# Reordering the tail of a two-block pair kernel: where the last triangle, the output gates and the scaled projection stand

## The reference, cut to what matters

```python
zn = _sparse_norm(z, alpha_in, beta_in)
a = sigmoid(_lin(zn, W_ga, b_ga)) * _lin(zn, W_la, b_la)
b = sigmoid(_lin(zn, W_gb, b_gb)) * _lin(zn, W_lb, b_lb)
k = jnp.einsum('bitc,bjtc->bijc', a, b)
kn = _sparse_norm(k, alpha_o, beta_o)      # one mean, one variance over all of k
return sigmoid(_lin(zn, W_go, b_go)) * _lin(kn, W_lo, b_lo)
...
x = x + _L1_conv_ref(_gn(x), ...)
```

## Time and profile before

| what | value |
|---|---|
| median of three runs | 309.21 us (308.65 to 311.91) |
| time of the profiled execution | 310.55 us |
| its span in the profile | 308.5 us |
| PE / DVE / ACT / POOL busy, share of the span | 80% / 77% / 69% / 64% |
| matmuls and other instructions in all | 8141 |

### The profile page before, as it was taken

The page is one execution under the profiler, slowest core; times in us unless marked ns, Lnnn a source line. Parts: engine busy times, 40 slices in busy tenths (PEclk is TensorE's granted clock), DMA queues, the critical chain, the costliest instruction groups (busy, mean ns, idle before and its releaser), DMA issues.

```text
span 308.5 us, 8141 instructions
## 1 busy us (share of the span) xinstructions
PE 246.4 (80%) x3337; PEld 145.8 (47%) x3342; DVE 237.5 (77%) x444; ACT 214.3 (69%) x393; POOL 196.4 (64%) x174
## 2 busy tenths in 40 slices
PE   3965774889799799799799799795972698979983
PEld 1442251464465455455455554563611245555662
DVE  3997979688998998998996896895867574422784
ACT  4766785699699689689688788593723366755390
POOL 8907888889989889889849727329085862000053
PEclk9995899899999999999999999998996599999999
DMA  7201022023031031031041033100000026455016
GB/s 245 67 0 55 16 78 62 0 62 78 2 102 36 2 97 45 3 102 36 2 104 36 0 100 83 29 2 3 0 2 0 1 50 149 128 140 146 12 50 222
DMA packets 32576, 18.14 MB, mean 59 GB/s; under 512 B 21084, under 2 KB 29596, under 8 KB 32540
## 3 DMA queue, kind: packets, MB, share of 16 engines
q1 hardware_dynamic: 32540, 17.63, 21.1%
HBM read 8.18 MB, written 5.77 MB: 45 GB/s over the span
## 4 chain that ended last, share of the span: by engine, by line
DVE 41%; PE 32%; ACT 11%; issue 6%; DMA 4%; POOL 3%; SPq 1%; DVEq 0%; ACTq 0%
PE PS L1181 29%; DVE t_sb L934 5%; DVE nmax L949 5%; DVE og L909 5%; DVE S_sb L953 4%; ACT u_sb L619 3%; DVE sums L870 3%; DVE gn_part L1018 2%; DVE Z L1171 2%; DVE PP L914 2%; ACT t_sb L633 2%; DMA k_dram<-og 2%; DMA x_tok<-in_x 1%; DVE xT L899 1%; DMA PP<-u_sb 1%
## 5 line engine op out<-in xcount | busy, mean ns | idle before, releaser
L1181 PE MATMUL PS<-znT,A_bd 128*128 128x512 f16 x192 | 49.1, 402 | 14.2 <-DVE t_sb L934 12.2
L440 POOL TENSOR_TENSOR S_sb<-S_sb,rden 128x512 f32<-128x512 f32 x32 | 35.5, 1132 | 24.3 <-DVE rden L889 24.3
L934 DVE TENSOR_TENSOR t_sb<-PS,t_sb 128x512 f16<-128x512 f32 x64 | 41.0, 685 | 10.7 <-ACT t_sb L633 10.7
L633 ACT CAST t_sb<-PS 128x512 f16<-128x512 f32 x64 | 36.3, 611 | 16.0 <-PE PS L1181 14.9
L446 POOL TENSOR_TENSOR PP<-S_sb,PP 128x512 f16<-128x512 f32 x32 | 36.5, 1159 | 6.5 <-ACT PP L627 6.5
L1181 PEld LDWEIGHTS PS<-znT,A_bd 128*128 128x128 f16 x192 | 17.6, 102 | 44.6 <-DVE t_sb L934 25.0
L1181 PEld LDWEIGHTS PS<-PP,Z 128*128 128x128 f16 x512 | 29.3, 114 | 12.9 <-issue 12.0
L619 ACT COPY u_sb<-PS 128x512 f32<-128x512 f32 x64 | 32.7, 613 | 1.7 <-PE PS L1181 1.7
L1181 PE MATMUL PS<-zbd,t_sb 128*128 128x64 f16 x768 | 26.6, 193 | 7.5 <-DVE t_sb L934 4.9
L1181 PE MATMUL PS<-PP,Z 128*128 128x128 f16 x512 | 31.4, 220 | 0.7 <-DVE S_sb L953 0.7
L1181 PEld LDWEIGHTS PS<-zbd,t_sb 128*128 128x128 f16 x768 | 23.8, 98 | 15.8 <-DVE S_sb L953 7.0
(11 more groups left out here) (204 smaller groups left out, 515.6 us busy)
## 6 DMA issues: line engine op xcount, KB each, us to landing
Z<-zn_dram SPq DMA_DIRECT2D x64, 64.0 KB, 2.9
x_tok<-in_x SPq DMA_DIRECT2D x4, 512.0 KB, 5.8
zn_dram<-zn_tok SPq DMA_DIRECT2D x8, 256.0 KB, 2.0
zbd<-znT SPq DMA_DIRECT2D x32, 64.0 KB, 2.0
out_x<-u_sb SPq DMA_DIRECT2D x4, 512.0 KB, 3.2
k_dram<-og SPq DMA_DIRECT2D x3, 512.0 KB, 4.6
th<-k_dram SPq DMA_DIRECT2D x12, 128.0 KB, 2.8
PP<-u_sb SPq DMA_DIRECT2D x8, 128.0 KB, 2.7
```

The source lines that it names most:

```text
L440: nc.gpsimd.tensor_tensor(P, P, bcast(rden[:, 32 * k:32 * k + 32], 2, N), ALU.mult).then_inc(p_nrm, 1)
L633: nc.scalar.copy(t_sb[:, HI, :, h], bank_tg(h)[:, :].rearrange("p (q i) -> p q i", i=N)).then_inc(t_hi, 1)
L934: nc.vector.tensor_tensor(t_sb[:, LO, :, h], bank_tg(h)[:, :].rearrange("p (q i) -> p q i", i=N), t_sb[:, HI, :, h], ALU.subtract).then_in ...
L1181: return nc.tensor.matmul(o, l, r, start=start, stop=stop)
```

## The change

PE's order becomes: triangle_last 0 and 1, gates 0 to 3, transpose_last, the sums, gates 4 to 7, then lo 0 to 7, then the transposes back. The gates use four banks in turn and are made in the order of `LO_ORDER`; their tanh is now written as it lies in the bank, (f, n, b), 512 columns side by side. One is added to it by POOL for units 0 to 3 and by DVE for units 4 to 7. Wlo_bd is multiplied by KS on DVE behind the k chain, and lo waits for that. DVE then forms (bank + CV) · (tanh + 1) straight from PSUM (`gated`), POOL adds x to all eight units while it turns (f, n, b) into (b, n, f), and PE waits for all eight units before it transposes the eight blocks back. Gone are `lo_evict`, `scale_k` and `fin_bank_x1`. ACT and DVE copy four result banks each.

```diff
+        bank_go = lambda n: PS[(0, 1, 2, 7)[n % 4]]
+        bank_lo = lambda n: PS[(5, 6)[n % 2]]
...
+        FIN_BANK = (0, 1, 2, 7, 3, 4, 5, 6)
+        ACT_OUT, DVE_OUT = (0, 2, 4, 6), (1, 3, 5, 7)
... (POOL)
-            for i in ADD_ORDER:
-                pool.wait_ge(lo_g, FIN_ORDER.index(i) + 1)
-                nc.gpsimd.tensor_tensor(fin(x2, i), fin(x2, i), fin(xT, i), ALU.add).then_inc(x2_ok, 1)
+            for n in range(4):
+                pool.wait_ge(go_th, n + 1)
+                v = fin(tg, n)
+                nc.gpsimd.tensor_scalar(v, v, 1.0, None, ALU.add).then_inc(tg_p[0], 1)
+            for n in range(A4):
+                pool.wait_ge(y_ok, n + 1)
+                nc.gpsimd.tensor_tensor(unit4(x2, LO_ORDER[n]), unit_ps(fin(tg, n)), unit4(xT, LO_ORDER[n]),
+                                        ALU.add).then_inc(x2_ok, 1)
... (ACT)
-            out_gates((0,))
             k_copy(6)
-            out_gates((1,))
             k_copy(7)
-            out_gates(range(2, A4))
-            act.wait_ge(k_ok, 7)
-            act.wait_ge(lo_ev, A4)
+            for n in range(A4):
+                act.wait_ge(go_mm, n + 1)
+                nc.scalar.activation(fin(tg, n), bank_go(n)[:, :], ACT.Tanh,
+                                     bias=col[:, BGH:BGH + 1], scale=0.5).then_inc(go_th, 1)
... (DVE: lo_evict and the old loop over FIN_ORDER go; behind kstep 7)
+            dve.wait_ge(k_ok, 5)
+            nc.vector.tensor_scalar(Wlo_bd[:, :, :], Wlo_bd[:, :, :], col[:, KS:KS + 1], None,
+                                    ALU.mult).then_inc(k_ok, 1)
+            def gate_plus(n):
+                dve.wait_ge(go_th, n + 1)
+                v = fin(tg, n)
+                nc.vector.tensor_scalar(v, v, 1.0, None, ALU.add).then_inc(tg_p[1], 1)
+            def gated(n):
+                dve.wait_ge(lo_mm, n + 1)
+                dve.wait_ge(tg_p[n // 4], n % 4 + 1)
+                nc.vector.scalar_tensor_tensor(out=fin(tg, n), in0=bank_lo(n)[:, :], scalar=col[:, CV:CV + 1],
+                                               in1=fin(tg, n), op0=ALU.add, op1=ALU.mult).then_inc(y_ok, 1)
+            dve.wait_ge(k_ok, 8)
+            for n in range(A4):
+                gated(n)
+                if 1 <= n < 5:
+                    gate_plus(n + 3)
... (PE)
+                    if n >= 4:
+                        pe.wait_ge(go_th, n - 3)
... (in lo)
-                        pe.wait_ge(pj_ok, 60)
+                        pe.wait_ge(k_ok, 8)
                     if n >= 2:
-                        pe.wait_ge(lo_ev, n - 1)
+                        pe.wait_ge(y_ok, n - 1)
... (PE's order)
             triangle_last(0)
             triangle_last(1)
+            out_gates(range(4))
             transpose_last()
             ...
+            out_gates(range(4, A4))
+            lo(range(A4))
+            pe.wait_ge(x2_ok, A4)
             for i in range(NS):
...
+                    last = nc.tensor.transpose(PS[FIN_BANK[i]][:, 128 * b:128 * b + 128], x2[:, at:at + 128], ident[:, :])
                 last.then_inc(x2_mm, 1)
```

More of the change, by code:

```diff
@@ L155, in build @@
         fin = lambda v, i: v[:, COLS * i:COLS * i + COLS]
-        unit_ps = lambda bank: bank[:, :].rearrange("p (f n b) -> p b n f", f=A4, n=2)
+        unit_ps = lambda v: v.rearrange("p (f n b) -> p b n f", f=A4, n=2)
         kT_u = lambda u: kT.rearrange("p (f m) -> p f m", f=A4)[:, :, 64 * u:64 * u + 64]
         z1_u = lambda p, u: z1[p][:, :, 2 * u:2 * u + 2].rearrange("p f n b -> p f (n b)")
-        bank_lo = lambda n: PS[(7, 2)[n % 2]]
+        bank_go = lambda n: PS[(0, 1, 2, 7)[n % 4]]
+        bank_lo = lambda n: PS[(5, 6)[n % 2]]
         out_tok = u_sb[:, :, :, :].rearrange("p h q i -> p (h q i)").rearrange("p (a b d) -> p a b d", a=A2, b=L)
@@ L253, in build @@
         k3_ok = sem("k3_ok")
-        lo_ev = sem("lo_ev")
         lo_mm = sem("lo_mm")
-        lo_s = sem("lo_s")
-        lo_g = sem("lo_g")
+        tg_p = [sem("tg_p0"), sem("tg_p1")]
+        y_ok = sem("y_ok")
         x2_ok = sem("x2_ok")
@@ L399, in _ @@
                 sp.wait_ge(x2_cp[0], len([m for m in ACT_OUT if m < i + 2]))
-                if i >= 4:
-                    sp.wait_ge(x2_cp[1], i + 2 - len([m for m in ACT_OUT if m < i + 2]))
+                sp.wait_ge(x2_cp[1], len([m for m in DVE_OUT if m < i + 2]))
                 sp.dma_start(out_dst[:, :, SB * D * i:SB * D * (i + 2)],
@@ L838, in out_copy @@
                                PS[FIN_BANK[i]][:, :].rearrange("p (b e d) -> p b e d", b=SB, e=A2)).then_inc(x2_cp[0], 1)
[L839 to L846, removed]
+            for i in ACT_OUT:
                 out_copy(i)
@@ L1141, in kstep @@
                 dve.wait_ge(k_ok, n)
[L1143 to L1147, removed]
             dve.wait_ge(ks_mm, 1)
@@ L1166, in _ @@
                                              col[:, BLH:BLH + 1], ALU.mult, ALU.add))
[L1167 to L1173, removed]
+            dve.wait_ge(k_ok, 5)
[15 more added lines that the diff above has]
+                    gate_plus(n + 3)
+            for i in DVE_OUT:
                 dve.wait_ge(x2_mm, i + 1)
@@ L1452, in _, with out_gates @@
             triangle(2)
[L1453 to L1460, removed]
+            def out_gates(ns):
+                for n in ns:
+                    if n >= 4:
+                        pe.wait_ge(go_th, n - 3)
+                    split_mm(bank_go(n)[:, :], [Wgo_bd[:, p].rearrange("p e d -> p (e d)") for p in (HI, LO)],
+                             [z1_u(p, LO_ORDER[n]) for p in (HI, LO)]
                              ).then_inc(go_mm, 1)
@@ L1492, in transpose_last @@
                         last.then_inc(k3_mm, 1)
[L1494 to L1500, removed]
             triangle_last(0)
-            lo((1,))
-            out_gates((1,))
             triangle_last(1)
-            out_gates((2, 3))
-            lo((2, 3))
+            out_gates(range(4))
             transpose_last()
```

20 lines of the change are left out of this document (removed).

## The result

The changed kernel takes 317.0 us (median of four runs, 314.43 to 318.45), beside 310.56 us for the kernel before (308.65 to 313.02); the ratio is 1.0216 with a 95% interval of 1.0157 to 1.0275. It is slower, by 1.6 to 2.8%. Forecast were 311.2 us, a range of 306.8 to 314.5, and "within 1%" as the likeliest. The profiled execution is the fastest of the four: 314.43, with a span of 312.7.

The account below looks back on a forecast made before the run. Old scaling and gating wait until all projections leave PSUM; in the new form POOL's eight additions take the gain back. First y 286.9, plus 11.6 and 0.8 gives 299.3, plus 11.2 gives span 310.5, median 311.2; range 306.8 to 314.5.

Parts of the forecast that it names:

- The sums 3.7 us earlier: PE's sums that open the k chain were to start at 281.33 in place of 285.04.
- the second half's 0.68: PE's second half of triangle_last was to take 1.41 us plus an unchanged pause of 0.68.
- The chain and the scaled weights: DVE's k chain was to take 2.86 us, the scaling of Wlo_bd 0.25, between 0.1 and 0.7.
- The start of POOL's additions: POOL was to be free at 286.3 and, with 0.4 us of blocking, have the first y at 286.9.
- about 0.85: POOL's cost in us for one addition of one, 512 columns; ends 0.5 and 1.56.
- the blocking is the bound: Rival: longer POOL and DVE alternation, or additions of one at 1.56 starting POOL at 289.1; median 313.4; chance 0.15.
- One addition of x, 1.45: Each of POOL's eight strided additions of x was to take 1.45 us; ends 1.14 and 1.9.
- The plain price of 1.14: Faster rival: POOL's additions of x cost 1.14 us each, as if steps were free; median 306.8; chance 0.12.
- DVE ahead of POOL: DVE's gatings, additions of one and waits were to take 12 us, staying ahead of POOL's additions of x.
- The drain, T + 11.2 with the fallen clock: Transposes, copies and stores were to end 11.2 us behind POOL's last addition at half clock, 10.1 without the fall.
- The signs of being wrong: Additions under 1.3 or over 1.6, pauses in POOL's row, first y before 285 or behind 288, drain outside 10 to 11.5.
- the first gating 8.2 us earlier: DVE's first gating, straight from PSUM, was to start at 285.8 in place of 294.00.

Follow-up runs that it names:

- e4: Changed kernel with gates 0 and 1 moved between the two halves of triangle_last; ratio 1.0139 to the kernel before.
- e1: Changed kernel with ACT, not POOL, adding one to the first four gates; ratio 1.0164 to the kernel before.
- e3: Changed kernel with 26 filler matmuls behind the last projection while PE waits for POOL; ratio 1.0228 to the kernel before.
- g1: Changed kernel with SP's second load of kT held until the last triangle is done; ratio 1.0109 to the kernel before, two executions only.
- f3: e4 plus: ACT adds all ones, projections write (b, n, f), gating writes x2, DVE adds x block by block; 307.54 us, ratio 0.9876 to the kernel before.
- f1: Changed kernel with the edits of e1 and e4 together; ratio 1.0090 to the kernel before.
- f5: f3 with the eight block-by-block additions of x on POOL instead of DVE; ratio 1.0027 to the kernel before.
- f2: e4 with POOL reading side by side: ACT reorders the gates and only the projections write in steps; ratio 1.0074 to the kernel before.
- e2: Changed kernel with projections and gates writing PSUM as (b, n, f), so POOL reads side by side; ratio 1.0224 to the kernel before.
- f6: Changed kernel with the edits of e1, e3 (17 fillers) and e4 together; ratio 1.0104 to the kernel before.

## Why the prediction was wrong, point by point

- **The sums 3.7 us earlier: wrong by 1.7.** The first step that failed is the second half's 0.68, "as the pause 'issue' of 0.68 came inside it and I know no reason for it to go". It grew, to 2.48: its place in the instructions stayed, and PE, without the two projections and two gates ahead of that place, came there 3.8 us behind the start of triangle 2 in place of 7.1. e4 took the pause back to 0.93 and the sums 1.2 us with it. The pause stood in the earlier trace rows, though the prediction has PE working without one from 274 to 297 us. What makes PE pause there stays open. In three of the four other profiled executions with the halves side by side there was more: the clock fell behind the pause and the next twelve matmuls took 1.7 us longer (e1, e3; g1 1.2).
- **The chain and the scaled weights: right.** 282.07 to 284.94, 2.87 us against 2.86; the scaling 0.52, where 0.25 was taken and 0.7 was the upper end, and 0.29 where POOL was idle (e1, f3). The first y stood 5.7 us behind the sums, 5.6 were forecast.
- **The start of POOL's additions: wrong by 1.9 us,** 7.4 us behind PE's start on the sums in place of 5.6. This is the second step that failed: the term "about 0.85" for an addition of one was 1.49 (5.89 for four). I had scaled a cast of 128 columns by its width, less 0.1 for what does not grow, a share that no row shows. The row of the same operation, POOL's TENSOR_SCALAR at 0.78 for 256 columns, gives 1.56 for 512, which I had only as an end of the range. The rival "the blocking is the bound", in its second half (additions of one at 1.56, start at 289.1), is what happened: 289.17, while the first y was there at 287.5. That the two times agree to 0.1 us is partly luck, as 1.7 us of late sums and a tail that began 1.3 us earlier stand against each other in it. e1 and f1 show that its removal gives 1.6 us.
- **One addition of x, 1.45: right,** 1.49 by median and 12.19 for eight with all blocking, where 12.4 stood. The rule of the Trainium skill (GPSIMD Engine Reference, Performance pitfalls for Q7 kernels), half as much again for steps over 8 bytes, is not borne out for this two-source form: 1.49 against 1.26 side by side (f5), 18%, and 1.27 in f2, where DVE works beside it as here. The plain price of 1.14 that I took from the blocked row was too low by 0.12.
- **DVE ahead of POOL: right.** No gap in POOL's row. DVE's additions of one took 1.05 to 1.53 beside POOL's additions of x, and 0.42 beside the last of POOL's additions of one. Three of POOL's eight additions took 1.68 to 1.70 and not 1.49, 0.6 us in all, where 0.8 was forecast.
- **The drain, T + 11.2 with the fallen clock: right,** 11.3 (T is the end of POOL's last addition); and T + 10.1 with the clock kept: 10.3 in e3.
- **The median.** The median before rose from 309.21 to 310.56 with a fourth run, which is 1.35 of the 5.8 us between forecast and result; the tail's terms above (1.7 for the sums, 1.9 for the start, 0.2 less for the additions with their blocking, 0.1 for the drain) make 3.5; the rest, 1.0, is not in the profiled execution, the fastest of the four. The clock behind the pause, which e1, e3 and g1 show and it does not, is large enough for it, and the mean granted clock of the four executions falls as their time rises: 0.941, 0.937, 0.928 and 0.926 at 314.43, 316.20, 317.81 and 318.45 us. Where in the span it fell is not shown, as no slower execution of this very kernel was profiled, and 1.0 us is also within the interval of the ratio (1.8 us to either side).
- **The signs of being wrong.** None of those that the prediction listed was met, as times within the span: an addition took 1.49, POOL's row had no pause, the first y came at 287.5, the drain took 11.3. (Counted from triangle 2, though, the first y would stand at 288.8, behind the 288 of the list.) The list watched the first y, the additions of x and the drain; of the two terms that failed, the pause and the additions of one, it had neither.

The gain that I saw, the first gating 8.2 us earlier, was there in part (286.78 - 271.15 = 15.6 us behind triangle 2, against 294.00 - 272.45 = 21.6: 5.9 us). It went into three things: POOL's twelve operations in a row on the path, stores that cannot start before the last of them, and the pause. f3's tail is 6.0 us shorter than e4's. Of that, f5 has 2.8, with the ones on ACT, the gating written straight to x2 and the blocks going out one by one, but x still added by POOL; 3.2 are the engine of the eight additions, and would be more without 1.1 us of half clock ahead of f3's sums. The early chain is worth something only once these are gone: f3.

## What to carry to other kernels

Take the price of a new instruction from a row of the same operation on the same engine, even at another size or stride, before you scale one of another operation; here that row was among those shown, and it was right within 5%. Moving work off a busy engine helps only if the engine that receives it does not become a serial row on the path: count that row from its first wait to its last instruction, and ask what could have left the chip in the meantime. In a reordering, a pause named "issue" may be tied to a place in the instructions: taking work out ahead of it can make it longer. And list signs of being wrong for every term of the sum, the small ones too.

## What the runs showed of the hardware that I had not expected

- POOL's TENSOR_SCALAR (one source, fp32, 512 columns side by side, in place) takes 1.49 us, more than its TENSOR_TENSOR addition of two such sources, 1.26 (f5). ACT does the same addition of one in 0.64 (2.55 for four in e1), DVE in 0.42.
- fp16 matmuls of 512 columns that write PSUM in steps of 16 elements have a pitch of 0.43 us in place of 0.22 at full clock (e2); fp32 ones keep theirs.
- PE pauses at one and the same instruction, the 171st matmul behind triangle 2, in all fourteen kernels here, 0.23 (f6) to 2.57 us (e3) long. The transfers of data beside it made no difference in the one run that held them back (g1).
- The clock can fall behind a pause of 2.4 us within dense work (e1, 2.39), and did behind 1.57 us of idle time in f3; behind 2.48 in the changed kernel's profile and 2.40 in e2's it did not. Executions of one kernel lie up to 4 us apart, and in the changed kernel the slower ones have the lower mean clock (0.941 to 0.926).
